# An attention layer gated by a mixture of experts: row filling, running sums and places moved to GpSimd, a longer stretch of attention ahead of the experts, and a small clear behind each scatter of results

## The reference, cut to what matters

```python
xn = _layernorm(x)                                   # x: (16, 256, 128), 4096 tokens
s = attention(xn)                                    # 16 heads of 8, one shared key and value head
g = _silu(ffn(xn))
out = x + s * g

# ffn: t = rmsnorm(xn) * norm_scale
logits = t @ gate_w + gate_b                         # 8 experts
top_v, top_i = jax.lax.top_k(logits, 2)
probs = jax.nn.softmax(top_v, axis=-1)
# each token goes through its two experts (128 -> 2*256 -> 128), the two results are
# weighted by probs, summed and added to xn
```

## Time and profile before

| | us |
|---|---|
| median of 3 runs | 525.67 |
| lowest and highest run | 521.95 and 539.46 |
| the profiled execution's own time | 526.86 |
| its span, first to last instruction | 525.1 |

### The profile page before, as it was taken

How to read it: one execution, slowest core, us unless ns; L and a number is a source line. 1 busy time by engine, 2 the same in 40 slices (tenths; PEclk the granted TensorE clock), 3 DMA queues, 4 the chain that set the end, 5 groups by cost and what they waited for, 6 DMA issues and landing times. The chain is left out here.

```text
span 525.1 us, 7730 instructions
## 1 busy us (share of the span) xinstructions
PE 402.5 (77%) x2375; PEld 245.6 (47%) x2375; DVE 300.5 (57%) x571; ACT 284.0 (54%) x640; POOL 215.6 (41%) x262
## 2 busy tenths in 40 slices
PE   3799879998701012699997698889889979999995
PEld 2677633443301000244443587778778863444321
DVE  6588789798400001458776256556545545889721
ACT  2635556987600001457776354455446446778893
POOL 4432550000777773500000045556546653448780
PEclk9999887998955555589999799999989997999998
DMA  6223452333211110131112456665656621543221
GB/s 173 76 76 104 152 172 59 126 112 128 95 51 51 56 51 25 64 119 49 45 50 85 117 148 161 167 179 166 187 159 166 161 74 34 161 132 102 82 74 31
DMA packets 51310, 55.40 MB, mean 105 GB/s; under 512 B 11747, under 2 KB 40291, under 8 KB 51142
## 3 DMA queue, kind: packets, MB, share of 16 engines
q1 hardware_dynamic: 46150, 45.45, 29.1%
q0 software_dynamic: 4544, 9.38, 5.2%
q10 hardware_dynamic: 576, 0.08, 0.1%
HBM read 34.46 MB, written 19.95 MB: 104 GB/s over the span
## 5 line engine op out<-in xcount | busy, mean ns | idle before, releaser
L1314 DVE TENSOR_REDUCE neg<-ps 128x4 f32<-128x1024 f32 x128 | 155.8, 1217 | 121.8 <-remote 70.9
L694 ACT ACTIVATE probs<-ps 128x512 f32<-128x512 f32 x256 | 142.2, 598 | 99.4 <-PE ps L843 40.9
L517 POOL DMA_INDIRECT y_dram<-early,xs x78 | 77.8, 997 | 141.6 <-ACT early L768 119.7
L843 PE MATMUL ps<-qs,k_stack 75*128 75x512 bf16 x256 | 96.6, 405 | 49.7 <-issue 29.0
L499 POOL DMA_INDIRECT sorted_dram<-rows,pos_i x64 | 61.7, 964 | 83.8 <-ACT rows L616 64.9
L858 PE MATMUL ps<-k_stack,qs 72*128 72x256 bf16 x512 | 90.7, 306 | 3.5 <-DVE neg L1314 3.4
L1007 PE MATMUL ps<-early,w_st 128*128 128x256 f32 x312 | 77.9, 394 | 15.4 <-ACT early L761 7.6
L843 PEld LDWEIGHTS ps<-qs,k_stack 75*128 75x128 bf16 x256 | 25.0, 99 | 126.0 <-ACT probs L694 60.2
L871 PE MATMUL ps<-probs,v_all 128*32 128x512 f32 x512 | 74.4, 656 | 0.0
L1390 DVE TENSOR_SCALAR early<-ps,b_st 128x256 f32<-128x256 f32 x78 | 34.2, 479 | 65.9 <-PE ps L1007 49.1
L1007 PEld LDWEIGHTS ps<-early,w_st 128*128 128x128 f32 x312 | 57.7, 195 | 25.6 <-issue 10.7
(11 more groups left out here) (147 smaller groups left out, 405.0 us busy)
## 6 DMA issues: line engine op xcount, KB each, us to landing
w_st<-in_w SPq DMA_DIRECT2D x39, 256.0 KB
qs<-q_dram SPq DMA_DIRECT2D x32, 288.0 KB
sorted_dram<-s_b SPq DMA_DIRECT2D x10, 520.0 KB, 5.2
xs<-sorted_dram SPq DMA_DIRECT2D x39, 130.0 KB
early<-y_dram SPq DMA_DIRECT2D x16, 256.0 KB, 7.5
q_dram<-early SPq DMA_DIRECT2D x16, 192.0 KB, 5.3
rows<-in_x SPq DMA_DIRECT2D x8, 256.0 KB
out<-rows SPq DMA_DIRECT2D x16, 128.0 KB, 2.2
```

The lines of the kernel that those rows point to most:

```text
L517: gp.indirect_dma_start(out=y_dram, out_offset=bass.IndirectOffsetOnAxis(ap=at[:, t, :], axis=0), in_=ys[:, r, t, :], in_offset=None).then ...
L694: sc.activation(probs[:, u % 2, k, :], ps[:, bank, :], ACT.Exp).then_inc(m["exp_ok"], 1)
L843: te.matmul(ps[:, bank, :], k_stack[0:KALL, at:at + P], qs[0:KALL, u % QS, j * 512:(j + 1) * 512], start=True, stop=True).then_inc(m["exp_ ...
L1314: ve.tensor_reduce(neg[:, b % 2, st, h:h + 4], ps[:, 3 + 2 * (n % 2):5 + 2 * (n % 2), :].rearrange("p a (e t) -> p (a e) t", e=2), AX, ALU ...
```

## The change

- `fill_row` moves from ScalarE to GpSimd (one multiply of 128 x 256 for each tile). Two tiles are filled before the first scatter, and behind the two scatters of tile t GpSimd fills tile t + 2.
- The running sums and the places of the tokens move from VectorE to GpSimd (`places`). VectorE keeps the counts, the first places (`first_places`), the shares (`shares`) and the experts of the blocks (`block_experts`), as separate parts hung behind the reductions of windows 7 to 9. `best_two` begins one reduction earlier. ScalarE copies the ranks in the middle of window 7 and writes the shifted start of the running sum.
- `EXPERTS_AT` is 21, so 25 windows stand ahead of the experts and 11 units behind them.
- Behind each scatter of results GpSimd clears 96 words of each partition of `kvg` and waits for that clear.
- The last keys move from window 6 to windows 12 and 13, the bias split from 5 to 13, the pads into windows 2 to 7, and the first `m_T` DMA from SP to ScalarE.

```diff
-EXPERTS_AT = 20
+EXPERTS_AT = 21
-KEYS_AT, LATE_KEYS_AT, ROUTE_AT, RANK_AT = 2, 6, 5, 7
+KEYS_AT, LATE_KEYS_AT, ROUTE_AT, RANK_AT, BIAS_AT = 2, (12, 13), 5, 7, 13
@@ SP @@
-                if w % 2 == 0 and 2 <= w <= UNITS:
+                if w % 2 == 0 and 4 <= w <= UNITS:
                     load_m(w // 2 - 1)
-                if 2 <= w < 12:
+                if w in (2, 3):
                     fill_pads(w - 2)
-                if w == 8:
+                if 4 <= w < 8:
+                    fill_pads(2 * w - 6)
+                    fill_pads(2 * w - 5)
+                if w == BIAS_AT + 2:
                     sp.wait_ge(m["bias_ok"], 1)
@@ GpSimd @@
+            def places():
+
+                pad, src = 16 * E, 0
+                pool.wait_ge(m["rank_sb"], 2)
+                for d in (1, 2, 4, 8, 16):
+                    link(gp.tensor_tensor(scan[:, 1 - src, pad:], scan[:, src, pad:],
+                                          scan[:, src, pad - d * E:pad - d * E + TILES * E], ALU.add))
+                    src = 1 - src
+                pool.wait_ge(m["base_ok"], 1)
+                link(gp.tensor_tensor(rt[3], scan[:, src, pad:], rt[1], ALU.add))
+                both = w2_sb[:, 4 * TILES * E:6 * TILES * E].rearrange("p (k c) -> p k c", k=TOPK)
+                mine = w2_sb[:, 6 * TILES * E:8 * TILES * E]
+                link(gp.tensor_tensor(mine.rearrange("p (k c) -> p k c", k=TOPK), both, replicated(rt[3], TOPK, 1), ALU.mult))
+                eight = mine.rearrange("p (t e) -> p t e", e=E)
+                four = rt[0].rearrange("p (t e) -> p t e", e=4)
+                two = halves.rearrange("p (t e) -> p t e", e=2)
+                link(gp.tensor_tensor(four, eight[:, :, 0:4], eight[:, :, 4:8], ALU.add))
+                link(gp.tensor_tensor(two, four[:, :, 0:2], four[:, :, 2:4], ALU.add))
+                at = rs[:, 8:10, :].rearrange("p k t -> p (k t)")
+                link(gp.tensor_tensor(at, two[:, :, 0], two[:, :, 1], ALU.add))
+                gp.tensor_copy(pos_i[:, :, :], rs[:, 8:10, :].rearrange("p k t -> p t k")).then_inc(m["pos_ok"], 1)
+                pool.wait_ge(m["pos_ok"], 1)
+
+            def fill_row(t):
+
+                gp.tensor_tensor(rows[:, t, :, 0:D], replicated(xn_all[:, t, :], TOPK, 1),
+                                 replicated(rms[:, t:t + 1], TOPK, 1).to_broadcast([P, TOPK, D]), ALU.mult
+                                 ).then_inc(m["row_ok"], 1)
+
@@
-            pool.wait_ge(m["route_ok"], 1)
+            pool.wait_ge(m["r_ok"], 1)
+            pool.wait_ge(m["kv_sb"], len(CHUNKS))
+            fill_row(0)
+            fill_row(1)
+            places()
             pool.wait_ge(m["p_ok"], 2)
             pool.wait_ge(m["pad_in"], 160)
             for t in range(TILES):
                 scatter(t)
+                if t + 2 < TILES:
+                    fill_row(t + 2)
@@
                 for t in range(2):
                     gp.indirect_dma_start(out=y_dram, out_offset=bass.IndirectOffsetOnAxis(ap=at[:, t, :], axis=0),
                                           in_=ys[:, r, t, :], in_offset=None).then_inc(y_out[r], 16)
+                    link(gp.memset(kvg[:, 0:4, :], 0.0))
@@ ScalarE @@
-            def fill_row(t):
-                if t == 0:
-                    act.wait_ge(m["r_ok"], 1)
-                sc.activation(rows[:, t, :, 0:D], replicated(xn_all[:, t, :], TOPK, 1), ACT.Copy,
-                              scale=rms[:, t:t + 1]).then_inc(m["row_ok"], 1)
@@
+                act.wait_ge(m["rank_sb"], 1)
+                sc.activation(scan[:, 0, at:], w2_sb[:, 0:(TILES - 1) * E], ACT.Copy).then_inc(m["rank_sb"], 1)
@@
+                if b == 0:
+                    act.wait_ge(m["mT_sb"], 1)
+                    act.dma_start(qs[KROWS:KALL, 0:2, :], m_T[:, 0, :]).then_inc(m_in[0], 16)
@@ VectorE @@
-            routing = [best_two(), sorted_places()]
+            routing = [best_two(), shares(), first_places(), block_experts()]
@@
-                    if w == 5 and r == 0:
+                    if w == BIAS_AT and r == 0:
                         biases()
-                    if w == ROUTE_AT and r == 0:
+                    if w == LATE_KEYS_AT[0] - 1 and r == 1:
                         key_rows(2)
-                    if w == ROUTE_AT and r >= 1 or w == ROUTE_AT + 1:
+                    if w == ROUTE_AT or w == ROUTE_AT + 1 and r < 2 or w == ROUTE_AT + 2 and r < 2:
                         route(0, 2)
-                    if w == ROUTE_AT + 2 and r == 0:
-                        while not route(0, 1):
-                            pass
-                    if ROUTE_AT + 2 < w <= ROUTE_AT + 6:
-                        route(1, 2)
-                if w == ROUTE_AT + 6:
-                    while not route(1, 1):
-                        pass
+                    if w == RANK_AT and r == 2:
+                        route(1, 3)
+                    if w == RANK_AT and r == 3 or w == RANK_AT + 1 and r < 2:
+                        route(2, 3)
+                    if w == RANK_AT + 2 and r >= 1:
+                        route(3, 2)
```

More of the change, by code:

```diff
@@ L90, in ring_items @@
         items += [("q", c)]
+    if w == RANK_AT:
+        items += [("rank", 0)]
     items += exps[4] + exps[5]
@@ L98, in ring_items @@
         items += [("keys", 1), ("keys", 2)]
-    if w == LATE_KEYS_AT:
-        items += [("keys", 3), ("keys", 4)]
-    if w == RANK_AT:
-        items += [("rank", 0)]
+    if w in LATE_KEYS_AT:
+        items += [("keys", LATE_KEYS_AT.index(w) + 3)]
     if w % 2 == 0 and 2 <= w <= UNITS:
@@ L216, in build @@
         cmp_s = scratch[:, 1600:1600 + EB]
+        counts = nt[:, 5, 0:E]
+        halves = scratch[:, 1344:1472]
         st6 = scratch[:, 1640:1640 + TILES * 6].rearrange("p (t c) -> p t c", c=6)
@@ L227, in build @@
             max_ps max_ok mpart mT_ps mT_sb m_in0 m_in1 exp_ps exp_ok pv_ok oT_sb oT_ps inv_ok on_ok onT_ps onT_sb s_ps s_ok
-            oh_ok rank_ps rank_sb e_ok e_exp p_ok route_ok pool_c row_ok scat
+            oh_ok rank_ps rank_sb e_ok e_exp base_ok pos_ok p_ok route_ok pool_c row_ok scat
             xs_in0 xs_in1 xs_in2 xs_in3 xs_in4 xs_in5 xs_in6 xs_in7 w_st0 w_st1 w_st2 xsT_ps xsT_sb h_ps glu_ok lin_ok top_ok hid_ok y_ps y_ok
@@ L265, in released @@
             return {"exp": (m["exp_ok"], n + 1), "mT": (m["mT_sb"], n + 1), "onT": (m["onT_sb"], n + 1),
-                    "s": (m["s_ok"], n + 1), "keys": (m["kst_sb"], n + 1), "rank": (m["rank_sb"], n + 1),
+                    "s": (m["s_ok"], n + 1), "keys": (m["kst_sb"], n + 1), "rank": (m["rank_sb"], 1),
                     "xT": (m["xT_sb"], n + 1), "q": (m["q_sb"], n + 1), "kv": (m["kv_sb"], n + 1)}[kind]
@@ L418, in attend @@
                 if w == 14:
+                    sp.wait_ge(m["pos_ok"], 1)
                     sp.wait_ge(m["route_ok"], 1)
@@ L713, in attend @@
                     evac_q(c)
+                if w == RANK_AT:
+                    evac_ranks()
                 exps(u, 4, 6)
@@ L724, in attend @@
                     evac_keys(2)
[L725 to L729 removed]
+                if w in LATE_KEYS_AT:
+                    evac_keys(LATE_KEYS_AT.index(w) + 3)
                 if w % 2 == 0 and 2 <= w <= UNITS:
@@ L732, in attend @@
                 exps(u, 7, 8)
-                if 6 <= w < 14:
-                    for t in range(4 * (w - 6), 4 * (w - 6) + 4):
-                        fill_row(t)
-                if w == RANK_AT:
+                if w == RANK_AT - 1:
                     act.wait_ge(m["e_ok"], 1)
@@ L964, in attend @@
                     queries(c, 1)
+                if w == RANK_AT:
+                    ranks()
                 scores_exp(u, 4)
@@ L977, in attend @@
                     turn_keys(2)
-                if w == LATE_KEYS_AT:
-                    turn_keys(3)
-                    turn_keys(4)
-                if w == RANK_AT:
-                    ranks()
+                if w in LATE_KEYS_AT:
+                    turn_keys(LATE_KEYS_AT.index(w) + 3)
                 if w % 2 == 0 and 2 <= w <= UNITS:
@@ L1147, in biases, with mark @@
                 ve.tensor_tensor(bias_parts[:, 2, :], bias_rest[:, :], bias_parts[:, 1, :], ALU.subtract).then_inc(m["bias_ok"], 1)
+            def mark(ins):
+                count[0] += 1
+                ins.then_inc(m["dve"], 1)
             def t3(i):
@@ L1220, in sorted_places, with first_places @@
+            def first_places():
+                tot = rt[0].rearrange("p (t e) -> p e t", e=E)
+                rank = rt[1].rearrange("p (t e) -> p t e", e=E)
+                dve.wait_ge(m["const_in"], 1)
+                dve.wait_ge(m["rank_sb"], 2)
+                mark(ve.tensor_reduce(counts, tot, AX, ALU.add))
                 yield
@@ L1231, in sorted_places, with shares, block_experts @@
                 yield
-                mark(ve.tensor_tensor(t3(6), t3(5), over_t(nt[:, 5, 8:16]), ALU.add))
```

(18 more changed lines are left out.)

51 lines of the change are left out of this document (9 added, 42 removed).

## The result

The changed kernel takes 457.55 us (median of 4, 455.11 to 460.22) where the kernel before, in runs taken beside it, takes 528.2 us (521.95 to 539.46). The ratio is 0.874, with a 95% interval of 0.863 to 0.885: 13% faster, 14.6 us over the forecast and inside its range. The profiled execution took 460.22 us, with a span of 458.2. A ratio compares only those runs of each kernel that are in the faster of its two states, so it can differ from that of the medians beside it. The chip of this measurement is one that shows the stall. On another chip the change made the kernel slower, and the experiments tell of that.

What follows compares the result with a forecast made beforehand. The prediction took completions queuing behind GpSimd's back-to-back scatters to bound the kernel, costing four windows 75.0 us. Its terms sum to -83.2, from 526.86 to 443.7 us, stated as 443; range of 8 in 10: 422 to 500.

Steps and rivals of the forecast that it cites:

- A: Whole kernel: the forecast holds and the stall goes, 443 us, within 425 to 470; chance 0.62.
- The stall: Windows 13 to 16: fills between GpSimd's scatters, 1.65 us a scatter, bring back all the lost time, -75.0 us.
- What remains of it: Windows 9 to 24: signals still wait a third of a us a window, +5 us (0 to +16).
- Windows 5 to 12: Early attention windows: VectorE's steps move to GpSimd and ScalarE loses its fills, -7.5 us (-15 to 0).
- Does GpSimd finish in time?: Scatters of rows: start near 101 us, end at 205 to 213, hidden before window 25 at 215.5; 0 in the sum.
- Entry to the experts: Ahead of the experts: SP's loads wait behind `load_m`, so all 10.6 us stand bare, +5.9 us (0 to +6).
- The experts: Experts' stage: with clears 1.6 us a scatter, 3.3 a block, GpSimd the bound; -11.6 us (-22 to -1).
- rival D: Clear behind scatters of results too short or drawn in beside them: experts keep 143 us or lose 15; 455 to 470; chance 0.05.
- The rest: First `m_T` from ScalarE, ranks copy, bias DMA, and the tail losing one window: 0, tail at worst +3 us.
- Fills beside VectorE: Windows with fills: GpSimd's fills lengthen VectorE's SBUF operations by up to 0.8 us, absorbed by idle time; 0.
- B: Scatter-stage windows: half relief, a fill only behind two scatters, 9.5 us a window, 482 us; chance 0.20.
- C: Scatter stage: GpSimd's being at work blocks the others, so fills lengthen the stall; slower, 552 us; chance 0.13.

Runs made afterwards that it cites:

- the version with the double clear: The changed kernel with the clear behind each scatter of results of 192 words instead of 96; 437.12 us, ratio 1.010 to the kernel before, on the calm chip.
- the experiment: The kernel with all fills ahead of the scatters, each scatter of rows carrying 64 partitions instead of 128; 435.61 and 434.73 us, both on the calm chip.

## Why the prediction came out as it did

The time fell inside the range, and the likeliest case, A, is what the trace after shows, though not all of its signs: windows 10 to 20 stand 7.5 us apart where 6.7 to 7.3 were to show it, and in the experts ScalarE still waits for TensorE's finished results, 2.44 us at 367.09 with nothing named that ended it. Luck had a part: nothing in the prediction asks which chip the kernel runs on, and on the calm chip its forecast of a faster kernel would have been wrong. The terms:

- *The stall*, -75.0. Windows 13 to 16 give -70.9, which is the -75.0 less 4.1 us of lateness that belongs to the next term. That it is the work between the scatters is shown by the kernel with all fills first (1.0005); that it works by the distance is shown in part by the kernel before with clears alone. The pair was put at 3.3 us and is 3.08, because the fill takes 0.62 and not 0.67 us and the next scatter follows it in 0.17, where 0.30 stand between two scatters.
- *What remains of it*, +5. 4.1 us in windows 13 to 16 and 1.2 in 17 to 23 (48.05 us for seven, calm 46.8): 5.3.
- *Windows 5 to 12*, -7.5. Measured -0.7, and they begin 2.2 us later: 9 us off, as much as in the experts. VectorE's relief came as forecast where VectorE was the bound: window 5 went from 12.1 us, with VectorE busy for 11.8 of them, to 8.6, and windows 5 to 8 from 38.0 to 31.7. Windows 9 to 12 gave it back, 36.3 us for 30.7. Window 9 alone takes 12.1 us for 6.3, with TensorE's granted clock at 0.50 and TensorE busy for 12.9 of the 13 us from 103 to 116. The version with the double clear has the same work in this stage; in its trace, on the calm chip, the clock stays at the upper level, window 9 takes 7.6 us and all eight take 60.6, 8.1 less than in the kernel before:
```profile
71.07:131.63 60.56, 54.82 (x373) 24.58 (x373) 54.92 (x95) 42.11 (x83) 34.92 (x44) 1.00 0.40 144
```
So the step failed in leaving TensorE's clock out, not in counting VectorE's steps. What the low stretch cost is 4.6 us in window 9; in windows 10 to 12, 2.9 us longer than there, late updates count too. It isn't the change alone that decides whether the clock falls: the changed kernel's own trace on the calm chip has a mean of 0.90 in this stage and takes 65.4 us.
- *Does GpSimd finish in time?* Scatters start at 104.9 (101 was said) and end at 202.8 (205 to 213), 15 us ahead of the first reduction of window 24. So they are hidden, with more room than forecast: the extra unit isn't needed, as the version with `EXPERTS_AT = 20` shows.
- *Entry to the experts*, +5.9. Measured +5.8, by the named mechanism: `load_m` at 224.09, loads behind it. The gap halves when the window ahead is an odd one.
- *The experts*, -11.6. Measured -2.7 (-2.1 to the first score tile at 376.42, the end that the prediction took), the other large miss. The step said that a scatter and its clear take 1.6 us, 3.3 a block, and that GpSimd would be the bound. They take 1.45 us where GpSimd runs on, 2.9 a block:
```profile
264.29 0.96 POOL L559 DMA_INDIRECT y_dram<-early,xs  x1 [0.28 <-issue]
...
265.72 0.96 POOL L559 DMA_INDIRECT y_dram<-early,xs  x1 [0.28 <-issue]
```
That is less than the 2.95 us in which TensorE's blocks follow each other, so GpSimd isn't the bound; it waits 18.8 us inside the stage for ScalarE's results, which are themselves late: at 1.44 to 1.52 us 39 to 43% of the updates still come over 1 us late on stalling chips, with the double clear too. This is what rival D said of the experts; its condition was half met. The start costs 2.0 us more: the first scatter comes 15.6 us behind the first transpose and not 13.6, with a mean granted clock of 0.67 in between and not 0.80. (The prediction's terms, 13.6 + 115.5 + 2, also add to 131.1 and not 131.5.) Why 1.54 us suffices nearly in the attention and 1.52 us doesn't in the experts, beside about twice the DMA traffic (166 to 180 GB/s in most of its slices against 80 to 109 in the attention), wasn't tried apart; on the calm chip more traffic still, about 200 GB/s and more in most of the experts' slices, goes with 3 to 4% of late updates.
- *The rest*, 0. Measured -1.8 (the window moved ahead of the experts takes 6.7 us and had taken 8.8 behind them; the tail 0.3 more).
- *Fills beside VectorE*, 0. Held in the sum: on the calm chip windows 15 to 17 with fills between the scatters take 6.7 to 7.4 us each and VectorE's reductions, which read PSUM, 1.23 us, as in the kernel before. But its small operations in SBUF do lengthen. Of the 25 that split the row maxima between 104 and 206 us six, all beside a fill, take 0.33 to 0.65 us and the others 0.17 to 0.21, for example
```profile
131.74 0.65 DVE L1318 CAST m_parts<-neg 128x32 bf16<-128x32 f32 x1
147.01 0.18 DVE L1318 CAST m_parts<-neg 128x32 bf16<-128x32 f32 x1
```
By the exclusive lock (the Trainium skill, SBUF — State Buffer, section "SBUF: two separate sides") up to 20 us of it was the estimate above; such a lock would look like these six, and they add up to 1.8 us.

B falls (7.5 us a window, not 9.5). C falls: GpSimd computes between scatters and nothing stalls. What no case held is that the stall belongs to some chips: on the calm one the same change is worth +3%, for the most part by the very terms that were forecast as its costs (entry, longer windows, tail) with little on the other side.

## What to carry to other kernels

When all engines go quiet while one issues indirect DMAs back to back, and their waits are marked "issue" or "remote", put useful work of that engine between the DMAs (here 0.62 us behind each second scatter, 1.26 to 1.54 us on average) before looking at any other part; test it by moving that work away and nothing else. Give the granted clock of each stage a place in the sum. Time such a change on more than one chip and record which: a fix for a stall that only some chips have must cost nothing on the others, so keep its other parts (a later stage, extra clears) to what they earn alone. Where a stage is entered behind a transfer that another engine has to feed, count that queue's order at the seam: one window's difference was 6 us.

## What the runs showed of the hardware that I had not expected

- Chips differ by 100 us in this kernel (528 to 535 against 430 to 431), with the same packets of GpSimd's queue and nearly the same instruction times. The difference is in the arrival of semaphore updates while GpSimd scatters: 93% over 1 us late in the stalled stretch of the kernel before, under 1% in the stretches of row scatters traced on the calm chip.
- The dependence on distance is steep: 81 us for one window at 1.26 us, 16.3 at 1.44, 7.5 at 1.54, 7.2 at 1.63. The second of these is from the kernel before, the others from versions of the changed one, and each is one trace.
- It touches GpSimd's own updates too: its wait for its own clear was ended by the clear 12 times on a stalling chip, 74 times on the calm one, of 77.
- What the late updates queue behind (rows sent, their bytes, or the instruction) is open: the experiment met the calm chip twice.
- GpSimd's fills lengthen VectorE's operations of 0.18 us in SBUF to as much as 0.65 us, and leave its reductions out of PSUM at 1.23.
